# Layer 1's routed tiles: two 64-row halves, each with its own expert, in place of one expert's 128 rows

## What is computed

```
scores = sigmoid(x @ gate_weight.T); sc = scores + gate_bias
topidx = top 6 of the 32 experts, from the 2 best of 4 groups
tw     = scores[topidx] / sum * 0.2
routed = sum over the 6 of  tw * ((silu(x @ w_gate[e]) * (x @ w_up[e])) @ w_down[e])     w: 256x128, 256x128, 128x256
anchor = 0.1 * the same with 16 small experts of inner width 64, one for each token (topidx[0] // 2)
out    = x + routed + shared(x) + anchor
```

## Time and profile before

| | |
|---|---|
| median of 3 runs | 1017.7 us (1017.7 to 1021.64) |
| the profiled execution's own time | 1019.59 us |
| its span | 1017.9 us |
| mean granted TensorE clock | 0.912 of 2.4 GHz |
| TensorE matmuls busy | 882.3 us (87%) |
| VectorE, ScalarE, GpSimd busy | 655.8, 485.7, 538.0 us |

### The profile page before, as it was taken

One profiled execution on the slowest core, in us unless ns is written; L12 is line 12 of the kernel. 1 busy time (PEld: TensorE's weight loads), 2 busy tenths in 40 slices (PEclk: granted clock), 3 DMA queues, 4 the chain that ended last, 5 costly groups with the idle time before them and its releaser, 6 DMA issues. The chain is left out here.

```text
span 1017.9 us, 23153 instructions
## 1 busy us (share of the span) xinstructions
PE 882.3 (87%) x6360; PEld 660.4 (65%) x6360; DVE 655.8 (64%) x3235; ACT 485.7 (48%) x1594; POOL 538.0 (53%) x543
## 2 busy tenths in 40 slices
PE   5888888876999999796999999978999999999960
PEld 2666666654469889554676676745787877777730
DVE  2657766764145445436689999967565666666687
ACT  2776766754023333221576667421355555555520
POOL 1005555677524444499805556766555566556630
PEclk9888989986999999997799999779899999999965
DMA  9998521104579994465322222396778655545497
GB/s 324 349 377 288 201 74 61 40 22 152 181 248 318 319 313 141 172 252 195 110 110 81 92 81 98 128 394 248 232 228 262 178 151 156 159 139 151 118 412 250
DMA packets 114064, 198.53 MB, mean 195 GB/s; under 512 B 18712, under 2 KB 86381, under 8 KB 110866
## 3 DMA queue, kind: packets, MB, share of 16 engines
q1 hardware_dynamic: 83922, 138.27, 41.7%
q0 software_dynamic: 22944, 50.38, 13.4%
q10 hardware_dynamic: 7072, 8.40, 2.5%
HBM read 113.72 MB, written 98.72 MB: 209 GB/s over the span
## 5 line engine op out<-in xcount | busy, mean ns | idle before, releaser
L985 POOL DMA_INDIRECT buf<-R,RI x240 | 235.7, 982 | 232.8 <-ACT R L1137 127.0
L770 PE MATMUL PS<-R,XT 128*128 x632 | 154.2, 368 | 5.6 <-DVE XT L1607 5.6
L1021 POOL DMA_INDIRECT yb<-YT,DI x98 | 95.6, 975 | 92.9 <-DVE DI L1600 83.6
L315 PE MATMUL PS<-R 128*128 128x256 f32 (+2 forms) x352 | 118.4, 473 | 16.3 <-DMA R<-in_ctxT 10.2
L1607 DVE COPY XT<-PS 128x256 f32<-128x256 f32 x222 | 94.0, 424 | 47.0 <-PE PS L320 43.4
L770 PEld LDWEIGHTS PS<-R,XT 128*128 128x128 f32 x632 | 106.0, 197 | 13.8 <-issue 6.6
L786 PE MATMUL PS<-R,AT 128*128 (+1 forms) x316 | 101.0, 403 | 0.0
L315 PEld LDWEIGHTS PS<-R 128*128 128x128 f32 (+1 forms) x352 | 69.8, 216 | 47.8 <-issue 32.6
L1137 ACT ACTIVATE R<-R,MX 128x120 f32<-128x120 f32 x256 | 80.1, 387 | 37.9 <-DVE MX L1433 37.9
L1312 ACT ACTIVATE SL<-PS 128x128 f32<-128x128 f32 (+1 forms) x158 | 42.2, 267 | 113.5 <-PE PS L770 106.4
L1137 ACT ACTIVATE R<-PS,MX 128x120 f32<-128x120 f32 x256 | 71.6, 368 | 30.1 <-DVE MX L1433 28.9
(11 more groups left out here) (208 smaller groups left out, 1878.9 us busy)
## 6 DMA issues: line engine op xcount, KB each, us to landing
R<-in_ew SPq DMA_DIRECT2D x64, 384.0 KB, 5.2
BX<-buf SPq DMA_DIRECT2D x128, 140.0 KB
yb<-Z SPq DMA_DIRECT2D x16, 1024.0 KB
R<-yb SPq DMA_DIRECT2D x16, 1024.0 KB, 4.8
R<-buf SPq DMA_DIRECT2D x94, 140.0 KB
R<-in_w SPq DMA_DIRECT2D x8, 1536.0 KB, 12.0
R<-yb SPq DMA_DIRECT2D x8, 1536.0 KB, 10.4
buf<-Z SPq DMA_DIRECT2D x8, 1120.0 KB, 13.4
```

The costliest lines, as they stand in the source:

```text
L315: m = e.matmul(out_, left, right, start=(i == 0), stop=(i == len(pairs) - 1))
L770: x = e.matmul(PS[:, 2 + j % 2, 0:2 * wd], XT[:, j % 3, k, :], src[:, bass.ds(regs[j], 1), k * 2 * wd:(k + 1) * 2 * wd].rearrange("p a n - ...
L985: e.indirect_dma_start(out=(buf1 if l else buf0)[:, :], out_offset=bass.IndirectOffsetOnAxis(ap=RI[:, n % 6, k:k + 1].bitcast(U32), axis=0 ...
L1021: e.indirect_dma_start(out=yb[:, :], out_offset=bass.IndirectOffsetOnAxis(ap=DI[:, j:j + 1].bitcast(U32), axis=0), in_=(YTS0 if i < E0 els ...
```

## The change

A routed tile now holds two halves of 64 rows. Each half belongs to an expert of its own, and the segments are counted in halves: 12288/64 = 192, and up to one more for each of 32 experts, 224 halves in T1 = 112 tiles. 31 anchor tiles stay, 143 in all; one anchor comes after every three routed tiles behind the first 48, so ROUTED is 133 and 10 anchors are left behind it.

- **TensorE.** For a routed tile, gate and up become four matmuls of 256 moving columns and down becomes two. The first half's use 64 stationary columns and write PSUM partitions 0 to 63, the second half's the other 64 stationary columns and partitions 64 to 127. The transposes before and between use the whole array as before.
- **Weights of the second half.** The first half reads its expert's weights in place, by a register. The second's are copied first: VectorE copies 512 columns (`gate_copy`), ScalarE 256 columns (`down_copy`), for each routed tile.
- **Matches in fours.** `matches1` does four tiles with four VectorE instructions, where `matches` had three (two with a read of the accumulator) for each. It waits until four tiles are loaded.
- **Loads.** Two DMAs of 64 rows for a routed tile in place of one of 128, into eight buffers in H2T's place. Expert numbers are read into registers four at a time.
- **Pads.** Routed segments are padded with 64 rows in place of 128. 16 of the pads move from GpSimd to SyncE (now 16 before the first load, 4 before) and ScalarE (16, as groups of 6, 5 and 5).
- **Tables.** The same tables with other small instructions; the 768-element comparison falls away.

The core of the diff:

```diff
-T1 = 127
+T1 = 112
+HALF = 64
+NB1 = 8
+BATCH = 4
-AHEAD, EVERY = 48, 4
+AHEAD, EVERY = 48, 3
...
                     for k in range(2):
-                        x = e.matmul(PS[:, 2 + j % 2, 0:2 * wd], XT[:, j % 3, k, :],
-                                     src[:, bass.ds(regs[j], 1), k * 2 * wd:(k + 1) * 2 * wd].rearrange("p a n -> p (a n)"),
-                                     start=(k == 0), stop=(k == 1))
+                        cols = slice(k * 2 * wd, (k + 1) * 2 * wd)
+                        if routed(j):
+                            e.matmul(PS[0:HALF, 2 + j % 2, 0:256], XT[:, j % 3, k, 0:HALF],
+                                     W1[:, bass.ds(regs[j], 1), cols].rearrange("p a n -> p (a n)"), start=(k == 0), stop=(k == 1))
+                            x = e.matmul(PS[HALF:P, 2 + j % 2, 0:256], XT[:, j % 3, k, HALF:P], SS_[:, j % 2, cols],
+                                         start=(k == 0), stop=(k == 1))
...
+                    if routed(j):
+                        w.wait_ge("a_wd", copies(j))
+                        e.matmul(PS[0:HALF, 4 + j % 2, 0:256], AT[:, j % 2, 0:HALF],
+                                 W1[:, bass.ds(regs[j], 1), 512:768].rearrange("p a n -> p (a n)"), start=True, stop=True)
+                        x = e.matmul(PS[HALF:P, 4 + j % 2, 0:256], AT[:, j % 2, HALF:P], WDR[:, j % 2, :], start=True, stop=True)
...
-            for x in range(4):
-                pad(x)
+            for x in range(0, 16, 4):
+                pads(x, 4)
...
+                if routed(i):
+                    for g in range(2):
+                        e.dma_start(RX[HALF * g:HALF * g + HALF, i % NB1, :],
+                                    buf1h[bass.ds(rs[g], 1), :, :].rearrange("a p r -> (a p) r")).then_inc(S[arrival(i % NB1)], 16)
...
-            for x in range(16, 32):
-                r = e.value_load(PAD[0:1, x:x + 1], min_val=0, max_val=DUM_A * P)
-                e.dma_start(buf1[bass.ds(r, P), :], Z[:, :]).then_inc(S["pad_b"], 16)
...
+            def down_copy(j):
+                r = who.of(j)[0]
+                w.wait_ge(group_of(j), 16)
+                w.wait_ge("s_dn", 32)
+                e.copy(WDR[:, j % 2, :], W1[:, bass.ds(r, 1), 512:768].rearrange("p a n -> p (a n)")).then_inc(S["a_wd"], 1)
...
+            def gate_copy(j):
+                r = who.of(j)[0]
+                w.wait_ge(group_of(j), 16)
+                e.tensor_copy(SS_[:, j % 2, :], W1[:, bass.ds(r, 1), 0:512].rearrange("p a n -> p (a n)")).then_inc(S["d_gu"], 1)
+
+            def matches1(i):
+
+                n, b = min(BATCH, NTL - i), i // BATCH
+                for k in range(i, i + n):
+                    w.wait_ge(*landed(k))
+                rows = RX[:, i % NB1:i % NB1 + n, :]
+                e.tensor_tensor(MEQ[:, 0:n, :], rows[:, :, 256:264], TE[:, i:i + n].unsqueeze(2).broadcast_to([P, n, 8]),
+                                ALU.is_equal).then_inc(*dv.up())
+                w.wait_ge("dv", dv.n)
+                e.tensor_tensor(MDW[:, 0:n, :, :], rows[:, :, 264:280].rearrange("p j (c k) -> p j c k", c=2),
+                                MEQ[:, 0:n, :].unsqueeze(2).broadcast_to([P, n, 2, 8]), ALU.mult).then_inc(*dv.up())
+                if b > 1:
+                    w.wait_ge("a_yt", E0 + BATCH * (b - 1))
+                w.wait_ge("dv", dv.n)
+                e.tensor_reduce(MS[:, b % 2, 0:n, :], MDW[:, 0:n, :, :], AX.X, ALU.add).then_inc(*dv.up())
+                w.wait_ge("dv", dv.n)
+                e.tensor_scalar(DI[:, i:i + n], MS[:, b % 2, 0:n, 0], OFF, None, ALU.add).then_inc(S["d_m"], 1)
...
             for i in range(NTL + 3):
                 if i < NTL:
                     xt_copy(E0 + i)
-                    w.wait_ge(f"bx{(E0 + i) % NBX}", 16 * ((E0 + i) // NBX + 1))
-                    matches(E0 + i, TE[:, ORDER[i]:ORDER[i] + 1])
+                    if i % BATCH == 0:
+                        matches1(i)
...
+                if i + 1 < NTL and routed(i + 1):
+                    gate_copy(i + 1)
```

More of the change, by code:

```diff
@@ L134 @@
     + [f"yl{i}" for i in range(3)] + [f"w1_{i}" for i in range(8)] + ["wa"]
-    + ["pad_s", "pad_t", "pad_a", "pad_b"] + [f"yf{i}" for i in range(4)] + [f"ya{i}" for i in range(4)]
+    + ["rx7"] + ["pad_s", "pad_t", "pad_a"] + [f"yf{i}" for i in range(4)] + [f"ya{i}" for i in range(4)]
     + ["p_z", "p_va", "p_set", "p_y", "p_xc"]
@@ L341, in all_back, with routed, landed, arrival @@
                 w.wait_ge(f"yt{s}", 16 * n)
+        def routed(i):
+            return ORDER[i] < T1
+        def landed(i):
+            s = i % NB1
+            loads = sum(2 if routed(k) else 1 for k in range(s, i + 1, NB1))
+            return arrival(s), 16 * (loads + (len(range(s, E0, NBX)) if s < NBX else 0))
+        def arrival(s):
+            return f"bx{s}" if s < NBX else "rx7"
+        def copies(i):
+            return sum(1 for k in range(i + 1) if routed(k))
+        def group_of(i):
+            return f"w1_{min((2 * ORDER[i] + 1) // 4, 7)}"
+        class Numbers:
+            def __init__(self, engine, table, sides, routed_most, anchor_most):
+                self.engine, self.table, self.sides, self.most, self.had = engine, table, sides, (routed_most, anchor_most), {}
+            def of(self, i):
+                o = ORDER[i]
+                kind, first, size = (0, 0, T1) if o < T1 else (1, T1, TA)
+                b = (o - first) // 4
+                if (kind, b) not in self.had:
+                    at = first + 4 * b
+                    self.had.pop((kind, b - 2), None)
+                    self.had[kind, b] = [
+                        nc.values_load_multi_w_load_instructions(
+                            self.table[HALF * g:HALF * g + 1, at:min(at + 4, first + size)], engines=[self.engine], min_val=0,
+                            max_val=self.most[kind], skip_runtime_bounds_check_because="the table holds minima with this bound",
+                            bass_reorder=False)[1]
+                        for g in ((0,) if kind else self.sides)]
+                return [v[(o - first) % 4] for v in self.had[kind, b]]
+        def pad_rows(engine, x, n):
+            return nc.values_load_multi_w_load_instructions(
+                PAD[0:1, x:x + n], engines=[engine], min_val=0, max_val=DUM_A * P,
+                skip_runtime_bounds_check_because="a count of at most 2048 behind the start of a segment", bass_reorder=False)[1]
+        def pad_height(x):
+            return HALF if x < R1 else P
         def width(i):
@@ L949, in yf_load @@
                 e.dma_start(YF[:, 2 * n:2 * n + 2, :], yv1p[:, 2 * n:2 * n + 2, :]).then_inc(S[f"yf{n % 4}"], 16)
-            for i in range(NBX):
+            for i in range(NB1):
                 bx1_load(i)
             for i in range(NTL + 3):
[L954 to L957, removed]
+                if i + NB1 < NTL:
+                    bx1_load(i + NB1)
+                if i in (10, 14):
+                    pads(R1 + (i - 10), 4)
                 n = i - ROUTED - 3
@@ L1277, in shared_behind @@
                 yield from pause(14)
-                for x in range(4, 8):
-                    pad(x)
+                pads(16, 6)
                 yield
@@ L1282, in shared_behind @@
                 yield from pause(2)
-                for x in range(8, 12):
-                    pad(x)
+                pads(22, 5)
                 yield from pause(5)
@@ L1287, in shared_behind @@
                 yield
-                for x in range(12, 16):
-                    pad(x)
+                pads(27, 5)
             ready1 = set()
@@ L1304, in _ @@
                     wa_load((i - 22) // 3)
-                if 10 <= i < 42 and i % 4 == 0:
-                    pad(R1 + 8 + (i - 12) // 4)
+                if i in (12, 16):
+                    pads(R1 + 8 + (i - 12), 4)
                 if 0 <= i - 1 < NTL:
@@ L1320, in _ @@
                     yt_out(E0 + i - 3)
+                if 0 <= i - 1 < NTL and routed(i - 1):
+                    down_copy(i - 1)
             for g in range(4):
@@ L1834, in tables @@
+                e.tensor_reduce(NUM[:, :, 2:3], CMA, AX.X, ALU.add).then_inc(*dv.up())
                 yield
                 w.wait_ge("dv", dv.n)
[L1836 to L1843 removed]
@@ L1861, in _ @@
+                if rest:
+                    e.tensor_copy(TE[:, end:end + rest], m[:, T1 - rest:T1]).then_inc(*dv.up())
+                e.tensor_scalar(TE[:, end + rest:NTL], m[:, T1 + mixed:NTL], float(R1), None, ALU.add).then_inc(S["d_tab"], 1)
             combine = y_add()
```

198 lines of the change are left out of this document (125 added, 73 removed).

## The result

The changed kernel takes 1063.34 us (median of 4 runs, 1062.41 to 1065.55) beside 1018.79 us for the kernel before in the same measurement: ratio 1.0436, 95% interval 1.0406 to 1.0466. It is slower by 44.6 us; forecast was +42.7 and 1060.4 us. In a later measurement the ratio was 1.0424 (1.0395 to 1.0452). The profiled execution took 1062.45 us.

A forecast was written before the change was run, and what follows sets the result against it. TensorE alone was taken to pace the expert stage, 1.63 us a routed tile. -24.4 + 65.0 + 3.1 + 0.5 - 1.5 = +42.7 us on the median of 1017.7 gives 1060.4; 80% range 1044 to 1090.

The forecast's parts named there:

- step 3: TensorE, routed tiles: going to halves and back costs 0.29 us, twice a tile, +65.0 us (+56.0 to +78.4).
- the row that spoke against it: Anchor's transpose with 64 stationary columns, next matmul after 0.11 us, no gap: would make the round-trip term 0, sum near 995.
- Step 1: Expert stage: 15 routed tiles fewer at 1.63 us each, -24.4 us.
- Step 2: Gate, up and down in routed tiles: both halves run together, 0 us; upper bound 1.30 us a tile.
- Step 4: Anchor tiles: 21 in place of 19 before the last routed result, 1.55 us each, +3.1 us.
- Step 5: `gate_copy` (0.68 us) and `down_copy` (0.42): VectorE at 1.74 and ScalarE at 1.33 a pass, hidden under 2.21.
- Step 7: Stage start: sixteen pads at 0.5 to 0.7 us, covered by 2 us; +0.5, up to 3 if cover is lost.
- Step 8: Stage end: six add turns with anchors before, four after, cheaper matches but one batch: -1.5 us (0 to -3).
- ScalarE's stalls: Expert stage, ScalarE behind its own DMA issues: grouped pads and longer passes pull opposite ways, 0 +-2 us.
- A: Rival, TensorE: 64 columns are no other division, no round-trip cost; 995 us, up to 1007 if VectorE-bound; chance 0.14.
- B: Rival, expert stage: gaps in every pass make TensorE's clock fall at times, some 15 us more, 1075; chance 0.08.
- C: Rival, routed tiles: halves do not run together, 146 us on top, 1206, or 1109 if partly; chance 0.05.

The follow-up runs named there:

- run 1: Changed kernel with gate, up and down of routed tiles as whole-array matmuls with the first half's expert, copies kept: 1011.17 us, ratio 0.9911.
- run 2: Changed kernel with only the down matmul of routed tiles on the whole array, gate and up still in halves: 1031.75 us, ratio 1.0101.
- run 4: Kernel before, 127 tiles and one load each, with only gate, up and down of routed tiles split into halves: 1096.37 us, ratio 1.0734.
- run 3: Changed kernel without `gate_copy`, `down_copy` and the waits for them, halves kept: 1062.48 us, ratio 1.0402.
- run 5: Kernel before with the anchors' down matmul on all 128 rows, the added weight rows zero: ratio 0.9975 to the kernel before.
- run 9: The edit of run 5 again on the kernel before, 12 runs beside 23: ratio 0.9963.
- runs 5 to 11: Anchors' down on 128 rows in the kernel before; reordered, combined or paired tiles in the changed kernel: ratios 0.9963 to 1.0225, kernel before at 1129 and 1144 us.

## Why the prediction was right

**The step that carried it** is step 3, two round trips a tile at 0.29 us: +65.0 for 112 tiles. Measured 0.298, +66.8. The partial sizes were right as well: 0.10 before the first half record, 0.05 at it, which I took for bare weight load (the record itself is 0.43 in place of 0.38), 0.10 and 0.05 on the way out; I had 0.09 + 0.024 and 0.09 + 0.05 from the rows of 32 columns, and some 0.04 on top for 64. Runs 1, 2 and 4 take it away or bring it in by itself: -52, -31.6 and +77.0 us.

**Why the row that spoke against it did not count**. The anchor's transpose with 64 stationary columns was followed without a gap, and by it the change would have won. After the change that form stands between half products: 852.47 to 852.78 (its start) is 0.31, so it pays the exit like any whole-array operation, and 0.23 later the halves pay the entry again. It is whole-array work with fewer columns. By the Trainium skill, page TensorEngine Tiling (Array Packing), Key Properties and Restrictions, a change of mode drains TensorE and transposes with float32 input are left out of column tiling; both agree with these starts. The page gives no duration; here the change costs 0.15 in and 0.15 out, and no run tells how much of that is the drain itself.

**Step 1,** -24.4: not separable in one run, but run 1 (15 tiles fewer at an undisturbed 1.63) and run 4 (127 tiles in halves, 33 us above the changed kernel; 15 x 2.22 = 33.3) show both prices of a tile, to within what their first passes and chance add. **Step 2,** halves side by side at 0: the starts lie 0.00 to 0.01 apart. **Step 4,** anchors, was a little high: +3.1, measured +2.3. An anchor makes three passes unlike a routed one, 1.51, 2.20 and 2.27, which is 1.53 us more than two routed passes; before it was 1.23 and 1.97, 1.57 more than one. 21 x 1.53 - 19 x 1.57 = 2.3.

**Step 5,** copies hidden: run 3. My bound of 0.68 for `gate_copy` was high, it takes 0.50. The remark that at 1.63 VectorE would be the bound came true in run 1 in a weaker form: it is not its sum but the batch of matches ahead of a product that holds the transpose up.

**Step 7,** the start, was mis-sized: +0.5, measured +1.8. I estimated a pad at 0.5 to 0.7 and a cover of 2 us. Sixteen pads took 13.62 us, 0.85 each with the register reads between them (13.84 in the second profile, where the totals came as in the kernel before: from 696.71 to 710.55, the first load at 712.31), and the chain goes through the last pad (712.13) and not through a scatter as before. The cover was gone, as the clause on its loss had it.

**Step 8,** the end: -2.0 against -1.5. The turns with anchors are 2.6 us (1018.56, 1021.14), those alone 2.1 (1028.10, 1030.22).

**ScalarE's stalls,** taken as 0 +- 2, gave -3.5: three passes of 2.66, 2.75 and 2.98 us in the trace before have no counterpart after. Runs 1 and 4 tell the longer pass from the regrouped pads: run 1 has the new groups with passes of 1.63, and the stall is there (2.42 us); run 4 has the old pads with passes of 2.22, and none of its passes is over 2.27 from 730 to 1040 us. The longer pass hides them.

**How the sum closes.** In the stage -24.4 + 66.8 + 2.3 - 3.5 = 41.2 against 40.6 measured in the first profile and 43.1 in the second, whose first passes ran longer at the lower clock. The total of 42.7 equals my sum, and that is partly luck: +1.8 on the trips, +1.3 on the pads and +2.3 of chance at the totals stand against -3.5, -0.8 on the anchors, -0.5 at the end and 0.6 that is left over. A term for the first passes at the lower clock was missing from the sum; it moved by over 2 us between the two profiles. By medians it was +44.6.

**The rivals.** A (64 columns are no other division) fell: passes 2.22, not 1.63. B (clock): granted clock 1.00 from 745 to 985, so the gaps between the starts did not lower it here; it is 0.50 only in the first passes, behind the wait for the first tile, as in the kernel before. C (halves in turn) fell by the starts.

## To carry to other kernels

Before you split an array into parts for more useful rows, count how often a pass goes from whole-array work (float32 transposes are that) to parts and back, and set some 0.3 us for each against what the split saves: here 0.22 us of tiles saved per tile left (24.4 / 112) against 0.60 paid. Put the parts' products together so that one round trip serves several, and check that operands made on other engines are ready at the new place. And read a fully busy engine by the distance of its starts, since a loss between two records that overlap is not idle time.

## What was not expected of the hardware

- A matmul on 64 of the 128 rows was dearer than the same matmul on all 128 with zeros, by 0.35 us where it stands between whole-array ones (runs 5 and 9).
- Weights of a half can be loaded while both halves multiply: 0.215 us between the records of a half, as on the whole array, with both weight loads in it (0.14 us each, at 854.22 and 854.23 in the changed kernel).
- A 128x512 float32 copy within SBUF on VectorE measured 0.41 to 0.69 us, median 0.43, mean 0.495.
- The slower condition of runs 5 to 11 cost 110 to 125 us of 1019 without changing an undisturbed pass (1.63). It took 57 us in layer 1's attention and under 1 in layer 0's experts (profile of run 5); the intervals of the ratios were 0.3 to 1.4% to either side.
- The same kernel was granted 0.50 of the clock in the stage's first passes from 719 to 722 us in one profile and from 717 to 726 in another, and its first four passes took 8.94 and 11.28 us.
